# Gelu's table load, the probabilities' copy and the down product change places in the windowed transformer

## The reference, cut to what matters

```python
def attn_layer(x, Wqkv, qs, ksc, Wo):
    q, k, v = heads of x @ Wqkv
    q = l2norm(q) * qs;  k = l2norm(k) * ksc
    q = q * cos * scale + rotate_half(q) * sin * scale
    k = k * cos / scale + rotate_half(k) * sin / scale
    return local_attention(q, k, v) @ Wo      # softmax over 64 keys per query
def ffn_layer(x, g, bln, W1, b1, W2, b2):
    xn = layernorm(x) * g + bln
    a, gate = split(xn @ W1 + b1)
    return a * gelu(gate) @ W2 + b2
for i in range(6):
    x = attn_layer(shift_tokens(x), ...) + x
    x = ffn_layer(shift_tokens(x), ...) + x
```

## Time and profile before

| | us |
|---|---|
| median of 3 executions | 3855.44 (3849.27 to 3860.63) |
| the profiled execution | 3847.89 |
| its span in the trace | 3846.1 |
| PE busy | 3488.5 (91%) |
| DVE busy | 2484.3 (65%) |
| ACT busy | 2288.7 (60%) |
| POOL busy | 1778.5 (46%) |

### The profile page before, as it was taken

The page is one execution under the profiler, slowest core; times in us unless marked ns, Lnnn a source line. Parts: engine busy times, 40 slices in busy tenths (PEclk is TensorE's granted clock), DMA queues, the critical chain, the costliest instruction groups (busy, mean ns, idle before and its releaser), DMA issues. The chain is left out here.

```text
span 3846.1 us, 125062 instructions
## 1 busy us (share of the span) xinstructions
PE 3488.5 (91%) x52643; PEld 2407.4 (63%) x52653; DVE 2484.3 (65%) x5535; ACT 2288.7 (60%) x4664; POOL 1778.5 (46%) x1846
## 2 busy tenths in 40 slices
PE   7996999999799997999999999999999996968885
PEld 4664555544466664676677677677677774846664
DVE  4446455510566655777777777777777774568885
ACT  2323655522455555777677777777777775457775
POOL 2003000000121126677676776776776773177773
PEclk9997999999799998999999999999999997989998
DMA  1000000010000002211221211221211211121100
GB/s 27 2 3 25 1 1 1 1 31 4 5 2 2 2 2 66 75 47 49 73 49 47 76 49 47 75 49 47 76 49 48 50 47 23 31 81 24 23 22 21
DMA packets 156331, 130.10 MB, mean 34 GB/s; under 512 B 53592, under 2 KB 146304, under 8 KB 154880
## 3 DMA queue, kind: packets, MB, share of 16 engines
q1 hardware_dynamic: 155776, 122.09, 12.3%
HBM read 31.93 MB, written 3.54 MB: 9 GB/s over the span
## 5 line engine op out<-in xcount | busy, mean ns | idle before, releaser
L1072 PE MATMUL t_wa<-t_w_qkv,t_resid 128*128 128x512 f32 x1152 | 584.5, 608 | 21.7 <-DMA t_scales<-in_L_ffn_k_scale 19.0
L1334 DVE TENSOR_REDUCE t_ssq<-t_sq 128x8 f32<-128x512 f32 x384 | 260.9, 679 | 134.4 <-ACT t_sq L1223 134.4
L1027 POOL TENSOR_TENSOR t_ra<-t_ra,t_rb 128x512 f32<-128x512 f32 x192 | 244.0, 1271 | 194.5 <-DVE t_rb L1352 194.5
L1223 ACT ACTIVATE t_sq<-t_wa 128x512 f32<-128x512 f32 x384 | 226.6, 590 | 151.3 <-PE t_wa L1072 151.3
L3109 DVE TENSOR_REDUCE a_nmax<-a_A 128x2 f32<-128x1024 f32 (+3 forms) x256 | 206.1, 823 | 127.0 <-PE a_A L3007 124.7
L1110 PEld LDWEIGHTS t_T<-ident,t_ra 128*128 128x128 f32 x1536 | 177.2, 141 | 145.0 <-issue 135.3
L1389 DVE TENSOR_REDUCE t_nmax<-t_S 128x8 f32<-128x512 f32 x192 | 132.8, 691 | 196.9 <-PE t_S L1094 189.2
L1072 PEld LDWEIGHTS t_wa<-t_w_qkv,t_resid 128*128 128x128 f32 x1152 | 188.3, 197 | 109.8 <-issue 94.4
L1110 PE MATMUL t_T<-ident,t_ra 128*128 128x128 f32 x1536 | 239.3, 279 | 14.5 <-ACT t_qT L1250 10.2
L1024 POOL TENSOR_TENSOR t_ra<-t_ra,t_rb 128x512 f32<-128x512 f32 x192 | 244.4, 1273 | 15.1
L3102 POOL TENSOR_SCALAR_AFFINE_SELECT a_pt<-a_pt 128x512 f32<-128x512 f32 x128 | 79.7, 634 | 370.1 <-ACT a_pt L3082 370.1
(11 more groups left out here) (506 smaller groups left out, 9747.6 us busy)
## 6 DMA issues: line engine op xcount, KB each, us to landing
t_vw<-t_vn SPq DMA_DIRECT2D x768, 66.0 KB, 2.0
t_vw<-t_vn SPq DMA_DIRECT2D x672, 33.0 KB, 2.3
t_w_qkv<-in_L_ffn_Wqkv SPq DMA_DIRECT2D x6, 1536.0 KB, 6.6
t_v<-t_vn SPq DMA_DIRECT2D x56, 132.0 KB, 2.9
t_vw<-t_nothing SPq DMA_DIRECT2D x96, 33.0 KB, 2.3
t_w_o<-in_L_ffn_Wo SPq DMA_DIRECT2D x6, 512.0 KB
f_h<-t_L_ffn_h_w SPq DMA_DIRECT2D x2, 1024.0 KB, 7.4
t_w<-in_L_ffn_W SPq DMA_DIRECT2D x6, 341.0 KB
```

What stands on the lines that cost most here:

```text
L1027: pool.tensor_tensor(ra[:, ahead % 2, 0], ra[:, ahead % 2, 0], rb[:, ahead % 2, 0], ALU.add).then_inc(q_added.sem, 1)
L1072: pe.matmul(bank, resid[:, b, lo:lo + P], w_qkv[:, l % 2, at:at + 512], start=True, stop=True).then_inc(wa_up.sem, 1)
L1223: act.activation(sq[:, r].rearrange("p h d -> p (h d)"), wa[:, WA[kind], :], ACT.Square).then_inc(squared.sem, 1)
L1334: v.tensor_reduce(ssq[:, n % 2, 8 * r:8 * r + 8, 0], sq[:, r], X, ALU.add).then_inc(summed.sem, 1)
```

## The change

Three pieces of order change, all in `transformer32`; no operation is added, removed or resized.

1. The load of gelu's table moves from the head of `gelus` to right behind `norm_turned`, and so ahead of the copy of the outputs.
2. In even slots ACT copies the transposed probabilities ahead of squaring the keys.
3. In even slots PE transposes the probabilities ahead of the down product.

```diff
@@ -1176,10 +1176,10 @@
                     if turn is not None:
                         turn_qk("q", turn)
                     if even:
+                        if now is not None:
+                            turn_p(now)
                         if last is not None:
                             down(last)
-                        if now is not None:
-                            turn_p(now)
                         if turn is not None:
                             turn_qk("k", turn)
                         if now is not None:
@@ -1262,7 +1262,6 @@
                 def gelus(t):
-                    act.preload_act_table_set("gelu_and_others")
                     l = layer_of(t)
                     bank = turned("gate", t)
@@ -1278,10 +1277,10 @@
                             square("q", ahead)
                         if turn is not None:
                             copy_q(turn)
+                        if now is not None:
+                            copy_p(now)
                         if ahead is not None:
                             square("k", ahead)
-                        if now is not None:
-                            copy_p(now)
                         if mid is not None:
                             copy_v(mid)
@@ -1307,6 +1306,7 @@
                             copy_k(turn)
                     if ffn is not None:
                         norm_turned(ffn)
+                        act.preload_act_table_set("gelu_and_others")
                     if now is not None:
                         copy_o(now)
                     if ffn is not None:
```

## The result

| | before | after |
|---|---|---|
| median of 5 executions, us | 3855.44 (3844.07 to 3860.63) | 3810.89 (3804.42 to 3814.89) |
| the profiled execution, us | 3847.89 | 3814.89 |
| its span, us | 3846.1 | 3813.1 |
| granted clock of PE over the span | 0.962 | 0.959 |

The account below looks back on a forecast made before the run. A pair's loop through PE, ACT and DVE was taken as the bound, 17.76 us before and 17.57 after. Its 0.19 us over 96 pairs makes 18 us, so 3855.44 - 18 = 3837, range 3818 to 3858.

Parts of the forecast that it names:

- The load's move: On ACT, the table load fills a 0.63 us idle gap, so the exponentials start 0.74 us earlier.
- The copy of the outputs: On ACT, ends at 2825.01, ahead of the up product's start on PE at 2825.26; its lateness was costed at nothing.
- The down product's lateness: On PE, the down product ends 0.44 us later than before, leaving DVE idle about 0.6 us.
- the residual: DVE's step behind the down product, forecast to start at 2829.50, only 0.10 us earlier than before.
- The signs named for being right: Trace marks across ACT, PE and DVE, such as DVE's idle ahead of q's sums shrinking from 1.43 to about 0.7.
- the period of 17.57: Forecast length in us of the pair's loop after the change, against 17.76 before.
- Everything on DVE behind it keeps its distance: DVE's steps behind the residual were to follow its start unchanged, 0.10 us earlier.
- the second chain: From square q on ACT through DVE's sums and residual to the normalised keys, said to run 0.09 us behind the loop.
- the 0.09 of the scores' maximum: DVE's wait for the scores from PE, forecast to vanish, so that their maximum starts 0.19 us earlier.
- more than forecast: Rival, chance 0.08: the down product truly ends ahead of its modelled end; 0.35 us a pair, 3822, up to 0.74, 3784.
- The slower one: Rival, chance 0.06: the down product waits on PE for late exponentials; 0.19 us a pair lost, 3874.
- The price of a drain: On ACT, about 1380 ns beside each table load's 1283 ns, making the sum a loss; chance 0.01.

Follow-up runs that it names:

- the copy of p alone: Against the kernel before, only ACT's copy of the transposed probabilities was put ahead of squaring the keys in even slots; ratio 0.9921.
- PE's order alone: Against the kernel before, only PE's transpose of the probabilities was put ahead of the down product in even slots; ratio 0.9988.
- the load alone: Against the kernel before, only the load of gelu's table was moved to right behind `norm_turned`; ratio 0.9925.

## Why the prediction was wrong

**Right, and shown.** The load's move was to bring the exponentials 0.74 us nearer to the norm's scale, and did so by 0.74. The copy of the outputs delayed nobody. The down product's lateness is the new bound, with 0.56 us of idle on DVE where 0.6 was forecast, and the residual follows it by 0.04 to 0.05. The table load was done in 1.28 us with no drain behind it, also where a copy follows (it starts 1.29 us behind the load's start). The signs named for being right appeared, with DVE's idle ahead of the sums of q at 0.60 us where about 0.7 was expected, except for the period of 17.57: none of the others looked at DVE's way between the residual and the scores.

**The step that failed** is the sentence "Everything on DVE behind it keeps its distance", and with it, in the description of the second chain, "DVE back to back until the keys are normalised at 2834.08". The gap was the 0.16 us ahead of the heads' sum, behind the mixing of heads, and as the mixing came 0.79 earlier it closed. The mixing's end at 2833.40 follows from the earlier trace rows, and the heads' sum at 2833.44 stood in the timeline, though not in the earlier trace rows. The prediction walks from the outputs' division to the keys' normalisation over the three operations between them as if all touched, and the only wait behind the mixing that it prices is the 0.09 of the scores' maximum. The term is 0.16 us a pair, 15 us, and the copy of p alone shows it by itself.

**A term that was mis-sized** is the residual: 0.16 earlier, not 0.10. In the pair that the prediction follows PE took 1.71 us from gate to up product, in the one shown of the kernel after 1.65. Before the change this step lay beside ACT's chain and cost nothing, so its chance lateness did not belong in a loop that now runs through PE. Together: 0.19 + 0.16 + 0.06 = 0.41, and 0.02 of rounding. 96 x 0.43 = 41 us. The forecast's range ended at 3818, 7 us above the measured 3810.89; with these terms in it the sum would have been 3855.44 - 41 = 3814.

**The rivals.** The one that came nearest is "more than forecast", but not for its reason: the modelled end of the down product was right (the residual starts at 2763.72, 0.05 behind 2763.67). The slower one had its mechanism right and its size wrong, for the same overlooked slack: PE's order alone lengthens an undisturbed pair by 0.04, not 0.19. The price of a drain, from the Trainium skill (ScalarE: Activation LUTs, "What ACT_TABLE_LOAD costs"), did not appear: in the kernel after, the instruction behind each load starts 1.29 to 1.30 us behind the load's start.

**What remains of the difference between 17.33 and 17.42** can be read off by sorting the pairs of a trace (those under 18.6 us), though no kernel of its own tests it. PE's way from gate to up product varies between 1.65 and about 1.8 us in every kernel. In the kernel after, 39 pairs with less than 1.70 have a median of 17.34 us and 31 pairs with 1.76 or more one of 17.46. Before, the same two sorts have 17.83 and 17.84: there ACT's chain of table loads is the longer one and hides the step. With the copy alone it isn't hidden: the late pairs take 17.59 in place of 17.50. What spreads the pairs of before is another step with the scores in it, from the mixing to their maximum: 17.77 us where it takes less than 3.45 us, 17.84 where it takes more. With the load alone both steps count: 17.41 where both are short, 17.57 where both are long. Why the two steps vary the traces don't say.

## What to carry to other kernels

Before calling a stretch of an engine gapless, subtract the usual distance of each two neighbours from the one measured: a wait of 0.16 us that the timeline doesn't print was nearly as large as the whole gain forecast, 0.19. In a hand-ordered pipeline an order is worth what the bound of the moment lets it be worth: the copy's place gave 0.26 us a pair alone, nothing with the load moved, and 0.24 again once DVE's wait was filled. When a move leaves an engine waiting for a known time, look for one operation of that length to put in the gap; here it gave another 0.8%. And look at the few pairs that are unlike the rest: here the 83 ordinary pairs won 34.9 us and the other twelve gave back 1.5 of it.

## What the runs showed of the hardware that was not expected

A copy placed directly behind the load of gelu's table starts 1.29 us behind the load's start and takes its usual 0.60 us, so a table switch costs here what the record shows and only the overlap of about 0.12 us with its neighbour besides. The same PE step, six matmuls and 72 small ones, takes 1.65 us in the quickest pairs and up to 0.15 more in others at a granted clock of 1.00; no wait in the trace explains it. And behind a wait of PE of 1.89 to 1.90 us the granted clock fell to 0.50 in some pairs and stayed at 1.00 in others of the same trace, with 1.1 to 1.5 us between the two.
